# The router's products between the halves of the output projection, fewer VectorE steps between logits and mix, and a new table of slots

## The reference

```python
# first layer: attention in windows of 128 columns, 8 heads of 32 rows
q, k = Wq @ norm(x) + bq, Wk @ norm(x) + bk      # per window, 256 rows each
v = Wv @ ctx + bv
attn = softmax(where(mask > 0, q^T k / sqrt(32), -1e9))
x = x + tanh(g_xattn) * (Wo @ gelu(v attn^T) + bo) * mask
# second layer: router over 64 experts for each row of x, the best 8 kept
flat = norm(x).reshape(4096, 2048)
scores = softmax(flat @ router_weight.T + router_bias)
topk_w, topk_idx = top_k(scores, 8)
w_dense = zeros(4096, 64) with topk_w at topk_idx
x = x + tanh(g_ffn) * (flat * sum(topk_w) + w_dense @ expert_bias)
```

## Time and profile before

| | before |
|---|---|
| median of 3 runs | 1338.01 us (1337.15 to 1338.21) |
| the profiled execution, its time | 1336.13 us |
| its span in the trace | 1334.1 us |
| PE busy | 1278.6 us, 96% |
| DVE busy | 999.9 us, 75% |
| ACT busy | 900.9 us, 68% |
| POOL busy | 714.7 us, 54% |
| mean granted clock of TensorE | 0.995 |

### The profile page before, as it was taken

How to read it: one execution, slowest core, us unless ns; L and a number is a source line. 1 busy time by engine, 2 the same in 40 slices (tenths; PEclk the granted TensorE clock), 3 DMA queues, 4 the chain that set the end, 5 groups by cost and what they waited for, 6 DMA issues and landing times.

```text
span 1334.1 us, 37952 instructions
## 1 busy us (share of the span) xinstructions
PE 1278.6 (96%) x15341; PEld 1131.6 (85%) x15341; DVE 999.9 (75%) x1886; ACT 900.9 (68%) x1600; POOL 714.7 (54%) x663
## 2 busy tenths in 40 slices
PE   3899999999999999999999999999999999999986
PEld 3798898898888889798888889888888889979875
DVE  6578768797678966888678876879667896686666
ACT  4466776776686676766667677676668677776654
POOL 2466655456655665445663665545665466545520
PEclk9899999999999999999999999999999999999999
DMA  9231111621127111451114411162112711131003
GB/s 275 78 105 60 42 32 39 226 90 42 34 77 238 42 35 38 144 171 42 34 41 163 152 38 35 41 218 98 42 34 75 240 34 41 40 132 57 26 5 126
DMA packets 120620, 116.15 MB, mean 87 GB/s; under 512 B 11392, under 2 KB 88320, under 8 KB 120320
## 3 DMA queue, kind: packets, MB, share of 16 engines
q1 hardware_dynamic: 119584, 113.74, 27.3%
q10 hardware_dynamic: 864, 0.01, 0.0%
HBM read 80.06 MB, written 33.65 MB: 85 GB/s over the span
## 4 chain that ended last, share of the span: by engine, by line
PE 90%; ACT 4%; DVE 4%; issue 1%; DMA 1%; POOL 1%; ACTq 0%; SPq 0%; DVEq 0%; POOLq 0%
PE ring L293 10%; PE ring L294 9%; PE ring L295 9%; PE ring L410 5%; PE ring L378 5%; PE ring L412 5%; PE ring L411 5%; PE ring L369 4%; PE ring L309 4%; PE ring L308 4%; PE ring L310 4%; PE ring L332 4%; PE ring L392 4%; PE ring L425 4%; PE PR L437 3%; PE ring L474 2%
## 5 line engine op out<-in xcount | busy, mean ns | idle before, releaser
L293 PE MATMUL ring<-z_hi,wqk_hi 128*128 128x256 f32 x1024 | 297.9, 291 | 24.6 <-DVE z_lo L975 22.0
L1060 POOL TENSOR_TENSOR cx_lo<-cx,cx_hi 128x512 fp32r<-128x512 f32 x128 | 165.4, 1292 | 257.1 <-ACT cx_hi L611 257.1
L294 PE MATMUL ring<-z_hi,wqk_lo 128*128 128x256 f32 x1024 | 291.0, 284 | 0.0
L295 PE MATMUL ring<-z_lo,wqk_hi 128*128 128x256 f32 x1024 | 290.7, 284 | 0.0
L293 PEld LDWEIGHTS ring<-z_hi,wqk_hi 128*128 128x128 f32 x1024 | 197.7, 193 | 37.2 <-DVE wqk_lo L956 22.0
L810 DVE SCALAR_TENSOR_TENSOR xt<-ring,cst,mg 128x256 f32<-128x256 f32 x256 | 112.1, 479 | 142.9 <-PE ring L412 142.9
L794 DVE RECIPROCAL o<-ring 128x512 f32<-128x512 f32 x64 | 214.1, 3345 | 1.1 <-PE ring L378 1.1
L1054 POOL TENSOR_TENSOR z_lo<-z,z_hi 128x1024 fp32r<-128x1024 f32 x63 | 151.6, 2407 | 114.9 <-ACT z_hi L595 114.9
L294 PEld LDWEIGHTS ring<-z_hi,wqk_lo 128*128 128x128 f32 x1024 | 197.9, 193 | 0.0
L295 PEld LDWEIGHTS ring<-z_lo,wqk_hi 128*128 128x128 f32 x1024 | 197.7, 193 | 0.0
L1066 POOL TENSOR_TENSOR X<-X,xt 128x512 f32<-128x512 f32 x128 | 163.5, 1280 | 49.0 <-DVE xt L810 38.7
(11 more groups left out here) (143 smaller groups left out, 3035.1 us busy)
## 6 DMA issues: line engine op xcount, KB each, us to landing
cx<-in_ctx SPq DMA_DIRECT2D x128, 256.0 KB, 2.7
out_y<-X SPq DMA_DIRECT2D x128, 256.0 KB, 3.0
X<-in_x SPq DMA_DIRECT2D x112, 256.0 KB, 5.5
mg<-in_mask SPq DMA_DIRECT2D x64, 128.0 KB, 3.0
X<-in_x SPq DMA_DIRECT2D x8, 512.0 KB, 8.4
sel<-rows_d SPq DMA_DIRECT2D x256, 3.0 KB
X<-in_eb SPq DMA_DIRECT2D x2, 512.0 KB, 8.5
X<-in_wqT SPq DMA_DIRECT2D x1, 512.0 KB, 11.4
```

What stands on the lines that cost most here:

```text
L293: e.matmul(o, wqk_hi[:, t, cols], z_hi[:, t, :], t == 0, False)
L294: e.matmul(o, wqk_lo[:, t, cols], z_hi[:, t, :], False, False)
L295: last = e.matmul(o, wqk_hi[:, t, cols], z_lo[:, t, :], False, t == DT - 1)
L1060: e.tensor_tensor(cx_lo[:], cx[p % NC][:], f32(cx_hi[:]), ALU.subtract).then_inc(cxlo_g, 1)
```

## The change

There are three parts. First, the table of slots is new; its effect on the order is shown below. Second, on DVE the part of the logits that does not need the product is made earlier in a new step, c_base (shift times scale, times swb, plus the bias), so that c_top has one pass of four instructions over the product instead of two. Third, tanh(g_ffn) is no longer multiplied into the weights of each batch: it is multiplied once into the experts' biases eb2, and into the row's scale as gate. The four instructions that write w2 become one, and the inverse of the sum stands first in c_weights.

```diff
 SLOTS = dict(
...
-    norm2=25.25, L=33.5, LT=35.25, c_top=35.75, c_exp=39.25, c_w=41.25, wT=43, wt_hi=43.5, wt_lo=42.5, mix=44.5, m_gap=0.25,
+    norm2=25.25, c_base=28.75, L=33, LT=34.75, c_top=35.25, c_exp=36.75, c_w=40.75, wT=40, wt_hi=40.75, wt_lo=42, mix=44, m_gap=0.25,
...
@@ w_turn
-                e.wait_ge(w2_v, 4 * (b + 1))
+                e.wait_ge(w2_v, b + 1)
...
@@ scalar
-                    e.activation(eb2[:], ebst, ACT.Copy).then_inc(a_w, 1)
+                    e.activation(eb2[:], ebst, ACT.Copy, scale=cst[:, TF:TF + 1]).then_inc(a_w, 1)
...
+            def c_base(b):
                 if b == 0:
                     e.wait_ge(sm_rb, 16)
-                e.wait_ge(dm_v, 2 * b + 1)
+                    e.wait_ge(sm_small, 96)
+                e.wait_ge(dm_v, 3 * b + 1)
+                e.wait_ge(rstd2_g, b + 1)
+                e.tensor_tensor(dm[:], dm[:], ln2[:, 2, :], ALU.mult).then_inc(dm_v, 1)
+                e.tensor_scalar(gate[:], ln2[:, 2, :], cst[:, TF:TF + 1], None, ALU.mult).then_inc(dm_v, 1)
+                e.wait_ge(dm_v, 3 * b + 2)
+                for t in range(DT):
+                    last = e.scalar_tensor_tensor(out=lr[:, t, :], in0=swb[:], scalar=dm[:, t:t + 1], in1=rbb[:],
+                                                  op0=ALU.mult, op1=ALU.add)
+                last.then_inc(base_v, 1)
+
+            def c_top(b):
+                e.wait_ge(base_v, b + 1)
                 e.wait_ge(lt_pe, b + 1)
                 for t in range(DT):
-                    last = e.scalar_tensor_tensor(out=lr[:, t, :], in0=swb[:], scalar=dm[:, t:t + 1],
-                                                  in1=bank("LT", b)[:, t * NX:(t + 1) * NX], op0=ALU.mult, op1=ALU.add)
-                last.then_inc(dm_v, 1)
-                e.wait_ge(dm_v, 2 * b + 2)
-                e.wait_ge(rstd2_g, b + 1)
-                for t in range(DT):
-                    last = e.scalar_tensor_tensor(out=lg[:, t, :], in0=lr[:, t, :], scalar=ln2[:, 2, t:t + 1], in1=rbb[:],
-                                                  op0=ALU.mult, op1=ALU.add)
+                    last = e.scalar_tensor_tensor(out=lg[:, t, :], in0=bank("LT", b)[:, t * NX:(t + 1) * NX],
+                                                  scalar=ln2[:, 2, t:t + 1], in1=lr[:, t, :], op0=ALU.mult, op1=ALU.add)
...
             def c_weights(b):
                 e.wait_ge(ex_a, b + 1)
+                e.reciprocal(sc[:, :, 3:4], sc[:, :, 1:2]).then_inc(wm_v, 1)
                 e.wait_ge(sel_v, b + 1)
                 e.tensor_tensor(ex[:], ex[:], lr[:], ALU.mult).then_inc(wm_v, 1)
-                e.reciprocal(sc[:, :, 3:4], sc[:, :, 1:2]).then_inc(wm_v, 1)
-                e.wait_ge(wm_v, 6 * b + 2)
-                e.tensor_reduce(sc[:, :, 2:3], ex[:], AX.X, ALU.add).then_inc(wm_v, 1)
-                e.tensor_scalar(sc[:, :, 4:5], sc[:, :, 3:4], cst[:, TF:TF + 1], None, ALU.mult).then_inc(wm_v, 1)
                 if b:
                     e.wait_ge(wT_pe, b)
-                e.wait_ge(wm_v, 6 * b + 4)
-                for t in range(DT):
-                    e.tensor_scalar(w2[:, t, :].rearrange("p (a x) -> p a x", a=2),
-                                    ex[:, t, :].unsqueeze(1).to_broadcast([128, 2, NX]),
-                                    sc[:, t, 4:5], None, ALU.mult).then_inc(w2_v, 1)
+                e.wait_ge(wm_v, 5 * b + 2)
+                e.tensor_tensor(w2[:], ex[:].unsqueeze(2).to_broadcast([128, DT, 2, NX]),
+                                sc[:, :, 3:4].unsqueeze(3).to_broadcast([128, DT, 2, NX]), ALU.mult).then_inc(w2_v, 1)
+                e.tensor_reduce(sc[:, :, 2:3], ex[:], AX.X, ALU.add).then_inc(wm_v, 1)
...
```

More of the change, by code:

```diff
@@ L42 @@
 SLOTS = dict(
[L44 to L52, removed]
-    norm2=25.25, L=33.5, LT=35.25, c_top=35.75, c_exp=39.25, c_w=41.25, wT=43, wt_hi=43.5, wt_lo=42.5, mix=44.5, m_gap=0.25,
-    sx=44.75, sx_gap=1.5, x2=46.5, rl=54.75, rl_gap=1,
-    x_1=10.0, x_gap=3.75, bn1=66.75, bn1_gap=1.75, norm1=96.75,
+    rows=-13.75, z32=-26.75, z_hi=-18.5, z_lo=-18, q=-11, q_ev=-12, k=-9.25, k_ev=-6.75,
+    c_hi=-14, c_lo=-11.25, v=-10.25, v_ev=-8, v_gap=-4.75,
+    S=0, top=2.25, split=5.25, MT=8, mt_ev=8, ST=12.5, exp=15.75, DEN=20, PV=20.5, rc=18.75, on=20.75,
+    gelu=23.5, mg=5, ot_hi=24.5, ot_lo=24.75, WO=29.5, WO_gap=1.5, xt=31.5, x1=34.75, bn2=41,
+    h=35.25, hT=38.25, hT_gap=0.25, ht_hi=41.75, ht_lo=43.25, R=45.5,
+    norm2=25.25, c_base=28.75, L=33, LT=34.75, c_top=35.25, c_exp=36.75, c_w=40.75, wT=40, wt_hi=40.75, wt_lo=42, mix=44, m_gap=0.25,
+    sx=44.25, sx_gap=1.5, x2=46, rl=55.75, rl_gap=1,
+    x_1=10.0, x_gap=3.75, bn1=68.5, bn1_gap=1.75, norm1=96,
 )
@@ L142, in gated_block_kernel @@
         ex = sb("ex", [128, DT, NX])
-        w2 = sb("w2", [128, DT, 2 * NX])
+        w2 = sb("w2", [128, DT, 2, NX])
         t8 = sb("t8", [128, DT, 8])
@@ L149, in gated_block_kernel @@
         half = sb("half", [128, DT])
+        gate = sb("gate", [128, DT])
         acc = sb("acc", [128, 2])
@@ L194, in gated_block_kernel @@
             "bn2", "agg2", "neg2", "rstd2", "h", "hT", "hthi", "htlo", "R"))
-        l_a, lt_pe, dm_v, lg_v, t8_v, neg_v, mr_v, sel_v, ex_a, w2_v, ac_v = (sem(n) for n in (
-            "L", "LT", "dm", "lg", "t8", "neg", "mr", "sel", "ex", "w2", "ac"))
+        l_a, lt_pe, dm_v, base_v, lg_v, t8_v, neg_v, mr_v, sel_v, ex_a, w2_v, ac_v = (sem(n) for n in (
+            "L", "LT", "dm", "base", "lg", "t8", "neg", "mr", "sel", "ex", "w2", "ac"))
         wm_v, wT_pe, wthi_a, wtlo_v, mix_pe, sx_a, x2_v = (sem(n) for n in (
@@ L258, in gated_block_kernel @@
             for b in batch(t, C["LT"]):
-                take(("LT", b), t, C["c_top"] - C["LT"], dm_v, 2 * b + 2)
+                take(("LT", b), t, C["c_top"] - C["LT"], lg_v, b + 1)
             for b in batch(t, C["wT"]):
@@ L456, in w_turn @@
                     keep_on(bank("wT", b)[:], 20)
-                e.wait_ge(w2_v, 4 * (b + 1))
+                e.wait_ge(w2_v, b + 1)
                 for t in range(DT):
-                    last = e.transpose(bank("wT", b)[:, t * 128:(t + 1) * 128], w2[:, t, :], ident[:])
+                    last = e.transpose(bank("wT", b)[:, t * 128:(t + 1) * 128], w2[:, t, :, :].rearrange("p a x -> p (a x)"), ident[:])
                 last.then_inc(wT_pe, 1)
@@ L921, in input_norm @@
                 if b >= 2:
-                    e.wait_ge(dm_v, 2 * (b - 1))
+                    e.wait_ge(dm_v, 3 * (b - 1))
                     e.wait_ge(h_a, NU * (b - 1))
@@ L998, in _ @@
                     e.wait_ge(a_w, 6)
-                    e.tensor_tensor(eb2[NX:128, :], ebst[NX:128, :], f32(eb2[NX:128, :]), ALU.subtract).then_inc(v_w, 1)
+                    e.scalar_tensor_tensor(out=eb2[NX:128, :], in0=ebst[NX:128, :], scalar=cst[NX:128, TF:TF + 1],
+                                           in1=f32(eb2[NX:128, :]), op0=ALU.mult, op1=ALU.subtract).then_inc(v_w, 1)
                 for u in due(t, C["top"]):
@@ L1023, in _ @@
                         r_low(u, a)
+                for b in batch(t, C["c_base"]):
+                    c_base(b)
                 for b in batch(t, C["c_top"]):
```

11 lines of the change are left out of this document (6 added, 5 removed).

## The result

The changed kernel takes **1345.32 us** median (4 runs, 1341.78 to 1346.06), where the kernel before took 1337.90 beside it on the same chip: ratio 1.0052, 95% interval [1.0037, 1.0067]. It is slower by half a percent, where 1321.5 us had been forecast. The profiled execution took 1346.06 us, span 1344.2.

The account below looks back on a forecast made before the run. PE's own list and its standstills were taken as the bound. Seven mixes at 1.35 + 0.78 us (14.9), 0.8 for end frames and 0.7 for the last batch gave -16.4 us, to 1319.7, forecast 1321.5 us as median, range 1315 to 1332.

Parts of the forecast that it names:

- R: Router's four products, moved from behind the scores to between the output projection's halves: 0.20 us less a frame.
- hT: Turning of h on PE, moved from behind the maxima's turn to ahead of k's projection: 0.07 us more a frame.
- plain frame: Stretch from one unit's scores to the next without the mix or waits: from 18.33 to 18.20 us.
- The rival of half the gain: Each change between whole array and parts costs 0.10 us anywhere: 6.2 us less gain, 1327.7 us; chance 0.12.
- Do other engines keep up in a plain frame?: DVE, ACT and POOL keep up; the tight place, L410 waiting for ot_lo, keeps 0.2 to 0.3 us; nothing charged.
- The frame with the mix: Frame holding the mix products: 29.15 us against 29.26, as the mix begins sooner but takes all 32 products and R.
- So 15.3 stands, set by ACT: Mix begins 15.3 us after the scores, before 17.35, limited by ACT's chain; PE itself would reach it at 15.15.
- where DVE waits for WO anyway: c_base's steps move a frame earlier into DVE's idle time, taking 0.8 us off the stretch from logits to exponentials.
- The last batch: Router's steps uncovered at the end: -0.8 for L846, -0.8 for shorter c_weights, +0.9 for R's delay; -0.7 us.
- The sum: Whole run: 14.9 us over seven mixes, 0.8 for six more plain frames, 0.7 for the last batch; -16.4 us.
- that PE gains nothing from the router's path: Rival: router's path shrinks but PE's frame with the mix stays as long; 9.4 us less gain, 1331 us; chance 0.14.
- that an engine is late: Rival: POOL's ot_lo arrives late at L410, 0.27 us a frame or more; gain lost, up to 1354 us; chance 0.07.

Follow-up runs that it names:

- e1_R_back: The changed kernel with the router's products put back behind the scores and the turn LT behind the sums, all else kept; 1346.49 us, ratio 1.0073.
- e3_R_alone: The kernel before with only the router's products moved between the halves of the output projection; 1365.52 us, ratio 1.0206.

## Why the prediction was wrong

- **R and hT** (-0.20, +0.07): right. 18.16 against 18.20 us in every plain frame, 0.94 between the halves, 2.96 behind hT, and no charge at the step from scores to sums (1.88 us from scores to weighing). The rival of half the gain is out. hT was moved alone in no run.
- **"Do other engines keep up in a plain frame? DVE, ACT and POOL have the same order ... and I charge nothing."** This is the step that failed. I looked for engines that come too late and found one tight place, ot_lo, which held. I took DVE's durations as fixed, wherever POOL's instructions fall. They are not. Taking R away from behind the scores brings cx_lo 1.14 us nearer to the scores and under the split of the maxima: 193 ns become 866. In plain frames nothing came of it. I also followed PE's earlier arrival to ot_lo alone ("PE arrives 0.80 to 0.83 us sooner") and not to k, which has the statistics in front of it once a batch. The statistics frame lost 1.71 us by the two (0.81 for the stalled split and 0.94 for the statistics, by the runs), the norm2 frame 0.41, where the output projection waits 0.38 us for ht_lo. On DVE the norm's steps stand there between k and ht_lo, 1.18 us (372.67 to 373.85); before they stood ahead of k. No run moved them, so that this is the cause is not shown; neither the split nor c_base changes the frame.
- **The frame with the mix, "So 15.3 stands, set by ACT"**: failed too. The first part was near: the exponentials were to start 8.67 us behind the scores (L333 at 378.82); ACT's timeline has them at 9.01:

```profile
387.83 0.35 ACT L671 ACTIVATE ex<-lg,sc 128x64 f32<-128x64 f32 x1 [0.61 <-DVE sc L869]
...
393.54 0.60 ACT L678 ACTIVATE wt_hi<-ring 128x512 fp32r<-128x512 f32 x1 [0.58 <-PE ring L460]
```
  Then L787's 1.31 us under cx_lo: the weights are ready at 13.85, forecast 13.0. Then five small steps, one of them 1.15 under ot_lo, and k stand between w2 and wt_lo on DVE. I had followed ACT's list here, not DVE's. wt_lo begins at 16.64 and the mix at 17.47 instead of 15.3. From the mix to the next scores it is 13.12, forecast 13.6. Together 30.82 in that frame against 29.15; in most batches it is 30.6 to 30.7, with 1.13 us before the mix. w2 itself costs 0.69 us, as I took it.
- **c_base "where DVE waits for WO anyway"**: right in its effect, for a reason that I hadn't seen. It takes 3.1 us there (375.06 to 378.12) instead of 1.0, and PE loses 0.45 at the scores behind, which its next wait takes up.
- **The last batch** (-0.7): from the last scores to the end it is 60.7 us, before 62.8, better than forecast, but most of that is luck. Before's clock fell to 0.50 for some 3 us in that stretch (from 1295.8), the changed kernel's did not; with such a fall the runs with the earlier split and with cx_lo in halves take 62.2 there. That leaves 0.6 for the change, near the 0.7.
- **The sum**: 1.50 + 1.71 + 0.41 - 5 x 0.04 = 3.4 us a batch (mix, statistics, norm2, plain frames), 24 us over seven batches, of the 26.5 by which the span missed. One statistics frame of 21.42 us (+1.5, the fall of the clock told above) and the first frames (1.2 us later than before at the third scores, where I had -0.3; their granted clocks are 0.875 and 0.856, before 0.911 and 0.906) are more than the rest, and the last batch gives 1.4 back. Of the 3.4 us a batch, the runs tie some 1.8 to collisions (0.81 and 0.25 by the earlier split, 0.7 by the two steps behind wt_lo) and 0.94 to the statistics, whose order has nothing to do with GpSimd.
- **The rivals**: that PE gains nothing from the router's path, and that an engine is late, were both named, with 0.14 and 0.07. Neither had the mechanism. The loss was at a place where the prediction had no bound at all.
- Undone step by step, the loss goes 1345.3, 1338.1 (split), 1331.4 (statistics), 1327.9 (two steps); as ratios to the kernel before beside each, 1.0052, 1.0004, 0.9965, 0.9934. Of what still parts the last from the forecast (6.4 us, or 8.0 between the spans) most is the norm2 frame's 0.41 and some 0.6 in the frame with the mix, seven times each, 7 us.

## What to carry to other kernels

Before moving an instruction on one engine, read where VectorE's steps with SBUF inputs and GpSimd's instructions come to lie against each other in the new order: a 0.17 us step costs what is left of the GpSimd instruction. Fill the time of a GpSimd instruction with VectorE steps that read PSUM. And a collision costs only what its own chain can't absorb: clearing the largest here, 1.9 us, by moving its step onto another chain cost 7 to 8 us, while clearing one of 1.1 us was worth some 4.

## What the runs showed of the hardware that I had not expected

- A VectorE step over 4 to 16 elements a partition that starts under a GpSimd elementwise instruction ends 0.01 to 0.04 us behind it, whatever is left of it, up to 2.2 us; with the GpSimd instruction cut from 1.29 to 0.74 us it takes 0.73. This held for TENSOR_TENSOR, TENSOR_SCALAR and CAST from SBUF (1.31 us for 128x16), and not for steps with a PSUM operand nor for bn_stats (0.70 us at most). The exceptions are two steps of the first unit in nearly every trace (before: L784 at 37.80 and L788 at 38.33 us), which start 0.08 us into a GpSimd scaling of 128x256 (0.55 us) and take only 0.20. Wider ones take their own time behind its end: 0.28 us for 128x256 (L880), 0.55 for 128x512 (w2 in e1_R_back).
- The granted clock went to 0.50 for some 3 us behind a wait of 1.81 to 1.88 us on PE in six of seven batches, and in none of before's behind one of 1.55 to 1.63. The length of the wait doesn't settle it: in e3_R_alone it fell in four of six batches with a wait of 1.81, and in the changed kernel once in seven behind 1.53. Such a fall made a frame 1.3 to 1.5 us longer. Five filler products ahead of the mix kept it at 1.00 in all frames with the mix, and gave 7 to 8 us back.
- The step from the scores (products on 32 rows of the array) to the sums and weighing (32 columns) cost nothing that can be seen: the scores take 0.99 us up to what follows, with R behind them or the sums (357.02 - 356.03, 343.03 - 342.04), the sums 0.89 with R ahead of them or the scores. Yet taking R's full-array products out from between them saved 0.2 us a frame (0.21 in e3_R_alone).
